# Graph attention with layer norm: the next round's slot tables built after the first batches, chunks prepared three ahead

## What is computed

```python
row, col = (edge_index[0], edge_index[1])
messages = x[col]
gate = messages @ W_gate.T + b_gate
h = messages @ W_lin.T + b_lin
g = gate[:, 0]
seg_max = jax.ops.segment_max(g, row, num_segments=n)
e = jnp.exp(g - seg_max[row])
denom = jax.ops.segment_sum(e, row, num_segments=n) + 1e-16
attn = (e / denom[row])[:, None]
pooled = jax.ops.segment_sum(attn * h, row, num_segments=n)
return pooled @ W_out.T + b_out
...
x = _layernorm(x + _L0_gnn_ref(x, edge_index, ...), axis=-1)
```

## Time and profile before

| | us |
|---|---|
| median of 3 runs | 2495.72 (2492.99 to 2502.05) |
| the profiled execution | 2495.45 |
| its span in the trace | 2493.6 |
| POOL busy, share of the span | 1646.9 (66%) |
| DVE busy | 1684.8 (68%) |
| PE busy | 1273.3 (51%) |
| ACT busy | 666.5 (27%) |

### The profile page before, as it was taken

How to read it: one execution, slowest core, us unless ns; L and a number is a source line. 1 busy time by engine, 2 the same in 40 slices (tenths; PEclk the granted TensorE clock), 3 DMA queues, 4 the chain that set the end, 5 groups by cost and what they waited for, 6 DMA issues and landing times.

```text
span 2493.6 us, 29384 instructions
## 1 busy us (share of the span) xinstructions
PE 1273.3 (51%) x5845; PEld 1093.0 (44%) x5845; DVE 1684.8 (68%) x6877; ACT 666.5 (27%) x2160; POOL 1646.9 (66%) x1714
## 2 busy tenths in 40 slices
PE   6710455555555555474556445444544445445665
PEld 4500344544444444474545434443443344334552
DVE  8997787788778875686666645554555456544787
ACT  3320222322232223203324223222322232223106
POOL 1007577777777777777767777777777777777025
PEclk8755565556556656666666666666666566656668
DMA  3023122222222222233222222222222222222233
GB/s 134 1 105 79 39 52 54 54 56 54 54 53 55 54 63 55 56 109 105 56 45 56 55 54 55 56 55 55 54 56 55 55 54 56 55 54 54 83 111 103
DMA packets 92094, 156.63 MB, mean 63 GB/s; under 512 B 29177, under 2 KB 61285, under 8 KB 91415
## 3 DMA queue, kind: packets, MB, share of 16 engines
q0 software_dynamic: 53152, 110.66, 19.7%
q1 hardware_dynamic: 38040, 43.90, 5.2%
q10 hardware_dynamic: 732, 0.20, 0.0%
HBM read 134.36 MB, written 20.28 MB: 62 GB/s over the span
## 4 chain that ended last, share of the span: by engine, by line
POOL 45%; DVE 24%; issue 19%; PE 8%; DVEq 2%; ACT 1%; DMA 1%; SPq 0%; ACTq 0%; POOLq 0%
POOL ring L570 45%; DVE nodes_sb L1212 8%; PE bank L883 3%; DVE first_keys L1094 3%; DVE first_keys L1095 3%; DVE spread L1207 2%; DVE late_keys L1095 2%; DVE late_keys L1094 2%; PE bank L864 1%; PE bank L852 1%; PE bank L824 1%; DVEq L1201 1%; DVE stats L1281 1%; PE bank L792 0%; DVE late_keys L1276 0%
## 5 line engine op out<-in xcount | busy, mean ns | idle before, releaser
L570 POOL DMA_INDIRECT ring<-node_table,gather_at x1661 | 1591.3, 958 | 702.9 <-issue 504.4
L883 PE MATMUL bank<-ring,spread 128*128 x3712 | 786.3, 387 | 411.7 <-DVE nodes_sb L1212 331.2
L883 PEld LDWEIGHTS bank<-ring,spread 128*128 128x128 f32 x3712 | 703.7, 286 | 486.8 <-issue 485.9
L1207 DVE TENSOR_SCALAR spread<-iota_row,places 128x128 f32<-128x128 f32 x1856 | 565.2, 305 | 359.1 <-PE bank L883 333.3
L1212 DVE SCALAR_TENSOR_TENSOR nodes_sb<-nodes_sb,drops,bank 128x130 f32 x1856 | 646.3, 348 | 5.4 <-issue 3.0
L670 ACT ACTIVATE ring<-ring,weights 128x129 f32<-128x129 f32 x1664 | 496.3, 390 | 3.5 <-issue 0.4
L694 ACT ACTIVATE weights<-bank 128x40 f32<-128x40 f32 x42 | 8.5, 203 | 961.9 <-PE bank L845 961.9
L1177 DVE TENSOR_TENSOR_SCAN run_max<-pen,bank 40x128 f32<-40x128 f32 x42 | 17.3, 412 | 289.9 <-PE bank L831 289.9
L824 PE MATMUL bank<-ended,ones 40*128 40x40 f32 x376 | 85.4, 397 | 187.9 <-DVE ended L1048 187.9
L824 PEld LDWEIGHTS bank<-ended,ones 40*128 40x128 f32 x376 | 79.8, 311 | 197.7 <-issue 197.7
L1094 DVE TENSOR_TENSOR late_keys<-late_keys 128x256 f32<-128x256 f32 x291 | 122.2, 420 | 4.5 <-ACT late_keys L628 1.7
(11 more groups left out here) (171 smaller groups left out, 1112.1 us busy)
## 6 DMA issues: line engine op xcount, KB each, us to landing
ring<-node_table,gather_at POOLq DMA_INDIRECT x1661
ring<-kept_sums SPq DMA_DIRECT2D x14, 455.0 KB, 5.2
node_table<-ring SPq DMA_DIRECT2D x1, 6347.7 KB
nodes_sb<-in_x SPq DMA_DIRECT2D x10, 625.0 KB
kept_sums<-nodes_sb SPq DMA_DIRECT2D x2, 2600.0 KB
ring<-in_x SPq DMA_DIRECT2D x10, 448.0 KB, 6.0
out<-ring SPq DMA_DIRECT2D x10, 448.0 KB
k<-sorted_keys SPq DMA_DIRECT2D x126, 20.0 KB
```

The costliest lines, as they stand in the source:

```text
L570: pool.indirect_dma_start(out=chunk_rows[c % RING][:, t, :], out_offset=None, in_=table[:, :], in_offset=bass.IndirectOffsetOnAxis(ap=gath ...
L883: last = pe.matmul(tile_ps(slot), lhsT=spread[:, slot, :], rhs=ring[:, bass.ds(got[slot], ROW)], start=True, stop=True)
L1207: return dve.tensor_scalar(spread[:, slot, :], iota_row[:, :], places[r % 2][:, t:t + 1], None, ALU.is_equal)
```

## The change

- `SORT_AHEAD` goes from 104 to 64 late sort steps ahead of round 0, and chunk 2 is prepared behind the first 24 of them (`FIRST_AHEAD`), on VectorE, PE and ACT alike. The other 40 steps go into rounds 0 to 12.
- Set 0 is prepared three ahead, as set 1: round r prepares chunk r + 3. Round 16 prepares nothing any more.
- In rounds with a chunk, PE's `sum_ended(r + 1)` moves from the round's start to behind batch 1, and `choose_rows(r + 1)` from behind `choose_drops` to behind batch 3; VectorE's `place_slots(r + 1)` moves from behind the softmax to batch 3. That is the order of the rounds without a chunk.
- ACT weighs batch 0 ahead of `keep_drops`.
- `turn_softmax` waits for `places_ready` of the round, which is posted at batch 5 of the round before.

```diff
-SORT_AHEAD = 104
+SORT_AHEAD = 64
+FIRST_AHEAD = 24
...
-    if r + 2 < FIRST_CHUNK[1] + PREPS:
-        return r + 2
+    if r + PREPS < FIRST_CHUNK[1] + PREPS:
+        return r + PREPS
...
+                    act.wait_ge(weights_ready, c + 1)
+                    weigh_batch(c, 0)
                 keep_drops(r)
-                if c is not None:
-                    act.wait_ge(weights_ready, c + 1)
-                for b in range(min(6, many)):
+                for b in range(1, min(6, many)):
                     weigh_batch(c, b)
...
+                pe.wait_ge(places_ready, r + 1)
                 pe.nop(nofuse=True)
                 pe.transpose(gate_rows, chunk_rows[c % RING][:, :, ROW - 1], ident[:, :]).then_inc(gates_turned, 1)
...
-                    if chunk_of(r) is None and r + 1 < ROUNDS:
+                    if r + 1 < ROUNDS:
                         if b == 1:
                             sum_ended(r + 1)
...
                 if chunk_of(r) is not None:
-                    sum_ended(r + 1)
                     turn_softmax(r)
                 choose_drops(r)
-                if chunk_of(r) is not None:
-                    choose_rows(r + 1)
                 sum_slots(r)
...
-            for step in late_order[:SORT_AHEAD]:
+            for step in late_order[:FIRST_AHEAD]:
+                sort_step(*step)
+            prepare(2, 1)
+            for step in late_order[FIRST_AHEAD:SORT_AHEAD]:
                 sort_step(*step)
...
                 if chunk_of(r) is not None:
-                    place_slots(r + 1)
                     dve.wait_ge(weights_ready, chunk_of(r) + 1)
...
-                    if b == 3 and chunk_of(r) is None and r + 1 < ROUNDS:
+                    if b == 3 and r + 1 < ROUNDS:
                         place_slots(r + 1)
```

More of the change, by code:

```diff
@@ L134, in prepared_upto @@
 def prepared_upto(r):
-    return 2 + sum(prepared_in(q) is not None for q in range(r))
+    return PREPS + sum(prepared_in(q) is not None for q in range(r))
 def chunks_upto(r):
@@ L686, in _ @@
             copy_prep(1)
-            for step in turnings(late_order[:SORT_AHEAD]):
+            for step in turnings(late_order[:FIRST_AHEAD]):
+                copy_turned(*step)
+            copy_prep(2)
+            for step in turnings(late_order[FIRST_AHEAD:SORT_AHEAD]):
                 copy_turned(*step)
@@ L903, in _ @@
             turn_prep(1, 0)
-            for step in turnings(late_order[:SORT_AHEAD]):
+            for step in turnings(late_order[:FIRST_AHEAD]):
+                turn(*step)
+            turn_prep(2, 0)
+            for step in turnings(late_order[FIRST_AHEAD:SORT_AHEAD]):
                 turn(*step)
```

## The result

The changed kernel takes 2481.87 us (median of 15 runs, 2464.49 to 2485.23) against 2496.3 us before (15 runs, 2492.2 to 2508.36): a ratio of 0.9919 over all runs, 95% interval 0.9901 to 0.9936. It is faster, by 0.8% or some 20 us by the ratio and by 14.4 us from median to median, where 32.8 us were forecast. The range that was given, 2455 to 2477, is 0.9837 to 0.9925 of the 2495.72 us known then: the ratio lies inside it, near its upper end, and the median lies 5 us above it.

The account below looks back on a forecast made before the run. POOL's gathers were taken as the bound up to chunk 40's end, VectorE and PE after it. Savings of 17.7, 11.2 and 3.9 us sum to 32.8 off 2495.45, giving 2462.65, put at 2463; range 2455 to 2477.

Parts of the forecast that it names:

- Part 1: Ahead of round 0: preparing chunk 2 behind 24 sort steps removes POOL's whole wait before it, -17.7 us.
- Part 2: Rounds 0 to 12: the moved sort steps add 2.0 us a round but cost 0 on POOL's path.
- Rival D: Gathers beside sorting: each VectorE instruction stops a gather's descriptors for its length; bound 2481; chance 0.03 together with C.
- C: Chunk 2's preparation waits in a queue and isn't early; 15 us remain, 2480; chance 0.03 together with Rival D.
- Part 3: Rounds with a chunk: moved tables and earlier weighing gain 3.6 us per bound round with a preparation.
- Part 4: POOL's wait before chunk 21: earlier rounds gain 16.2 us, over the 11.2 needed, so -11.2 us.
- Rival A: Bound rounds: added tables cost PE their full 1.9 us, gaining about nothing; 2475.5; chance 0.13 for all or part.
- Part 5: The end, from chunk 40's gates: rounds 43 and 44 shorten, -3.9 us, between -1 and -5.
- Rival B: Sort rounds: turned keys come late and VectorE waits; 2.4 us per block cancels the gain; chance 0.04.

Follow-up runs that it names:

- e2: Kernel before with only the new sort split and the three-ahead preparation, tables and weighing in the old order: 2485.68 us, ratio 0.9944.
- e5: Changed kernel with drains behind every second sort step ahead of round 0 and between adjacent sort steps within rounds: 2462.39 us, ratio 0.9846.
- e3: Changed kernel with a VectorE drain behind every second sort step ahead of round 0: 2466.62 us, ratio 0.9873.
- e11: Changed kernel with e3's drains, and within rounds drains only between the sort steps behind batch 3: 2462.74 us, ratio 0.985.
- e1: Kernel before with only the new order of the tables and of batch 0's weighing: 2489.3 us, ratio 0.9957.
- e4: Changed kernel with 40 instead of 24 sort steps ahead of chunk 2's preparation: 2469.61 us, ratio 0.9898.
- e9: Changed kernel with ACT's old order, batch 0 weighed behind the drops: 2474.75 us, ratio 0.9907.
- e8: Changed kernel with 8 instead of 24 sort steps ahead of chunk 2's preparation: 2474.73 us, ratio 0.9896.
- e7: Kernel before with a drain behind every second of its 104 sort steps ahead of round 0: 2508.58 us, ratio 1.0025.
- e6: Changed kernel with a one-column copy, no drain, behind every second sort step ahead of round 0: 2475.04 us, ratio 0.9892.

## Where the prediction was right, and the step that failed

**Part 1, right in what it removed.** The wait before chunk 2 is gone, round 0 started at 262.03 (forecast 262), and nothing was late next on ACT, PE or VectorE. Yet chunk 2 started only 4.0 us earlier, at 309.18 against 313.20, since POOL itself came 13.7 us later. A wait was replaced by a hold.

**Part 2, the step that failed.** It put the cost on POOL's path at 0, and the slowing of the gathers at 0.3 us, from the average of 0.9 us a chunk. The runs showed 22.3 us in the profiled execution: one hold of 16.0 us, 7.2 us in chunks 2 to 12, mostly short holds, and 1.9 us in chunks 13 to 20 (25.1 us), less some 2.8 us by which the other gathers, most of them up to chunk 2, were faster than before. (Of the 1.9 us, 1.3 are the long fifteenth gather of chunk 13; but e2 and e5, which don't have it, lose 1.8 and 1.6 us in these chunks as well, so its cause stays open.) e3 takes away the hold at the price of its drains, and gives 15.3 us at the median; at a ratio of 0.9873 it is at the forecast's 0.9869. e5 and e11 take away the short holds too, and come out below it, at 0.9846 and 0.985. There are three errors in the step. First, an average of 0.9 us per chunk was spread evenly, while the cost is a rare event as long as the row of steps it falls into; the average was read in a trace where none had fallen. Second, "the steps moved ran beside gathers before as well" is true, but before, a loss of up to 17.7 us ahead of chunk 2 was free. The change took the 17.7 us wait and with it the cushion. Third, the move of the place tables was charged by its time alone. Its place put sort steps behind them with no product between, and gathers that start there are held: e1 has the move and the short holds, e2 has neither. A chunk's pace is (877.57 - 309.18) / 11 = 51.7 us, against 51.0. What did not fail is the length of the rounds. In after they take 50.5 to 53.9 us in rounds 2 to 12, and not 48.4, with scan waits of 2.3 to 5.7 us, because POOL is late and the gathers set the starts; in e3, where POOL is on time, rounds 0 to 7 take 48.0.

**Rival D, dismissed too cheaply.** It shared 0.03 with C, and its bound of 2481 is where the median came. That the numbers meet is chance: D charged VectorE's work in the 17.7 us in which POOL stood, and what came is one hold as long as 24 steps, 77 us ahead of that place, with short ones behind it; with 40 steps (e4) the upper group lies at 2493.6. Its mechanism was stated too strongly, since in most places VectorE's instructions beside a gather cost it nothing or 0.1 us (1.04 instead of 0.94 us in e4), and it priced a steady tax. What came is a rare and long hold: of two gathers in a row one takes 1.01 us and the next 16.93. The argument against it was an average, and an average can't speak on that. The Trainium skill (SBUF — State Buffer, section on SBUF's two separate sides) says that the port pair is locked for an instruction's length; it has GpSimd's descriptors locked out by VectorE's instructions in a 2-port mode, and lets those with two inputs in SBUF, as the sort steps are, block only GpSimd operations that read SBUF. The trace agrees in part: VectorE's work on two inputs holds a gather, and the hold ends when that work ends, but it spans some 46 instructions (218.75 to 234.24 at 0.335 us each) and not one. No run here shows which port or lock it is.

**Part 3, right.** The scan's wait of 2.42 us is gone. The wait for the first products is 5.10 (forecast 5.5), and the first two pairs lie 1154.92 - 1149.23 = 5.69 us apart (forecast 5.7, from round 16 alone; in round 17 of before they lay 1100.65 - 1093.85 = 6.80 apart, which the prediction left out). Bound rounds gained 3.2 to 3.7 us, with 3.6 forecast; e9 confirms that the row choice's move needs the weighing's. (The weighing's move alone was not tried.) In sort rounds the gain was real, 48.0 us a round in e3 with 48.4 forecast, but in after it lay behind the gathers.

**Part 4, right, with one size off.** The 11.2 us are gone. Round 16, which prepares nothing now, went from 28.6 to 25.6 us: 3.0 gained, where 0.5 was taken and 2.3 was the upper bound. Round 17 gained 1.4 and round 18 lost 1.0. Rival A didn't occur. e2, without the tables' move, kept 6.9 us of the wait, 4.3 less than before; e1, with it alone, kept none, so the tables' move is the half that does it. (POOL was 16 us late in e1, at 1290.38 instead of 1274.18, but so was round 19, by 15.3.) e9, with the old weighing, has 2.1 us of wait there.

**Part 5, right.** -4.7 us against -3.9 forecast, within -1 to -5: round 43 took 33.5 us instead of 34.5 and round 44 33.1 instead of 36.7. The first gather of chunk 41 lies one gather ahead of the row, and chunk 16's does as well (1.25 us, since chunk 15 has 39 tiles; it changes nothing).

**Rival B** didn't occur: VectorE's waits for turned late keys sum to 4.1 us in four places, 1.4 the longest (1.7 before). **C** didn't occur.

**The range** held 2455 to 2477, with the sum at 2462.65. It took in 2 us of gather pace and A, but not D's bound, though Part 2 had named 17.7 us as the end of its own cost. Had it been kept, 2481 would have been the upper end, 1 us short of the median. That the ratio lies inside the range is in part luck: the room up to 2477 was made for A, which didn't occur, and is filled by runs with and without a hold. The forecast is near for the runs that by their times have no long hold (2464.5 to 2470.4, 4 of 15) and off by 19 for the median.

**What stays open.** What decides whether the gather is held. In the traces, gathers that began 0.26 or 0.27 us after the row's first instruction passed (before, e3, e4, e9), and those that began 0.23 to 0.62 us after it were held (0.62 after, 0.61 e1, 0.24 e8, 0.23 e2), so the offset from the row's start alone doesn't separate them. A free gather with its gap takes 1.34 us there, four sort instructions of 0.335 us, so that a passing phase would repeat; this fits long rows in which all pass, but wasn't tested.

## What to carry to other kernels

A wait on the engine that bounds a kernel is also a cushion: before it is removed, ask what has been losing time unseen in front of it. An average slowing (0.9 us a chunk) says nothing of a rare event that is as long as the longest unbroken row of work beside it, so bound the cost by that row's length, and look at the spread of the runs, where two groups some 10 us apart were a hint (2492.99 and 2495.72 against 2502.05 already in the three runs of before). Where runs fall into groups, give the groups, since a median tells only which is larger. Where GpSimd issues gathers while VectorE does long rows of two-operand work, a break every second step was worth 15 us at the median here, if VectorE isn't what is waited for (in e7 52 such breaks made a wait 9 us longer).

## What the runs showed of the hardware

- A gather issued by POOL during an unbroken row of VectorE's operations on two operands in SBUF can be held for the whole rest of the row: 2.65 us in a row of six instructions, 6.58 us beside 8 sort steps, 16.93 and 17.31 us beside 24, 28.85 us in e1. It isn't so in every execution (by their times 11 of 15 in after, 2 of 12 in e4), and after has two groups of times with it and e3, whose row is broken up, has one.
- With a drain or a one-column copy of 0.14 us behind every second step, no gather in the row lasts over 1.3 us (e3) or 2.1 us (e6); a drain costs VectorE about 0.2 us (10 us for 52), and lets most gathers go as fast as alone (0.94 us).
- Six sort instructions behind the place tables hit the fifteenth gather of a chunk time and again in after, where the gathers set the rounds' starts. In e9, where no scan waits longer than 0.8 us up to round 13, the three short holds (2.0 to 2.9 us) are of a 24th, a 21st and an 18th gather.
